# Two-layer transformer on one core: the second attention's preparation reordered and left without scaled output products, and its first head's projections on six PSUM banks shared with VectorE

## The reference, cut to what matters

```python
x = x + _L0_attn_ref(_layernorm(x), ...)
x = x + _L0_ffn_ref(_layernorm(x), ...)
x = x + _L1_attn_ref(_layernorm(x), ...)      # the change is here
x = x + _L1_ffn_ref(_layernorm(x), ...)

def _L1_attn_ref(x, d_kv_w, d_kv_b, u_k_w, u_k_b, u_v_w, u_v_b, d_q_w, d_q_b, u_q_w, u_q_b, qr_w, qr_b, out_w, out_b):
    kv_c = _linear(x, d_kv_w, d_kv_b)
    k_c = _linear(kv_c, u_k_w, u_k_b).reshape(b, s, H, Dh)
    k_r = _linear(kv_c, qr_w, qr_b).reshape(b, s, H, Dr)
    v = _linear(kv_c, u_v_w, u_v_b).reshape(b, s, H, Dh)
    q_c_lat = _linear(x, d_q_w, d_q_b)
    q_c = _linear(q_c_lat, u_q_w, u_q_b).reshape(b, s, H, Dh)
    q_r = _linear(q_c_lat, qr_w, qr_b).reshape(b, s, H, Dr)
    q_r, k_r = _rope(q_r), _rope(k_r)
    q, k = concatenate([q_c, q_r]), concatenate([k_c, k_r])
    probs = softmax(einsum('bhqd,bhkd->bhqk', q, k) / math.sqrt(Dh + Dr))
    ctx = einsum('bhqk,bhkd->bhqd', probs, v)
    return _linear(ctx, out_w, out_b)
```

## Time and profile before

| | |
|---|---|
| time, median of 3 runs | 2518.01 us (2516.64 to 2523.02) |
| the profiled execution | 2521.48 us, its span 2520.2 us |
| mean granted clock of TensorE | 0.972 |
| busy, share of the span | PE 88%, DVE 85%, ACT 74%, POOL 43% |
| start of the preparation, first score, first exponential | 778.4, 867.4, 873.8 us |

### The profile page before, as it was taken

The page is one execution under the profiler, slowest core; times in us unless marked ns, Lnnn a source line. Parts: engine busy times, 40 slices in busy tenths (PEclk is TensorE's granted clock), DMA queues, the critical chain, the costliest instruction groups (busy, mean ns, idle before and its releaser), DMA issues.

```text
span 2520.2 us, 50461 instructions
## 1 busy us (share of the span) xinstructions
PE 2216.9 (88%) x18456; PEld 1584.6 (63%) x18544; DVE 2136.7 (85%) x3174; ACT 1854.4 (74%) x2639; POOL 1074.1 (43%) x1488
## 2 busy tenths in 40 slices
PE   5888888869997599999999999999999999988899
PEld 2444444445555366777777777777777767766587
DVE  6888888758985399999999999999999999988421
ACT  4777777736675388888888888888888888878411
POOL 3312112102222465665665665656656656632200
PEclk9999999979998599999999999999999999999899
DMA  3000000050000099999999999999999999999200
GB/s 126 1 2 2 1 1 2 2 114 1 1 1 1 10 183 187 194 190 193 195 192 190 193 192 192 194 191 193 195 191 191 196 187 193 196 200 196 49 17 17
DMA packets 1119317, 300.67 MB, mean 119 GB/s; under 512 B 1107232, under 2 KB 1116416, under 8 KB 1118208
## 3 DMA queue, kind: packets, MB, share of 16 engines
q1 hardware_dynamic: 1116224, 295.21, 67.4%
q10 hardware_dynamic: 2848, 2.23, 0.3%
HBM read 18.45 MB, written 2.10 MB: 8 GB/s over the span
## 4 chain that ended last, share of the span: by engine, by line
DVE 29%; PE 21%; issue 9%; ACT 4%; DMA 4%; POOL 0%; DVEq 0%; SPq 0%; ACTq 0%; POOLq 0%
DVE parts L1570 13%; DVE lows L1554 12%; DMA partsT<-parts 4%; PE psS L1501 3%; PE psOb L1421 3%; PE psS L1404 2%; PE psS L1406 2%; PE psS L1405 2%; ACT parts L1733 2%; PE psOb L1457 1%; ACT prob L1723 1%; PE psOb L1422 1%; PE psOb L1521 1%; PE psPb L1521 1%; DVE shift L1562 1%
## 5 line engine op out<-in xcount | busy, mean ns | idle before, releaser
L1723 ACT ACTIVATE prob<-psS,shift 128x1024 f32<-128x1024 f32 x512 | 574.4, 1122 | 177.2 <-DVE shift L1562 168.0
L1570 DVE TENSOR_TENSOR parts<-prob,parts 128x1024 f16<-128x1024 f32 x512 | 659.5, 1288 | 23.2 <-ACT parts L1733 20.3
L1554 DVE TENSOR_REDUCE lows<-psS 128x1 f32<-128x1024 f32 x512 | 621.4, 1214 | 8.8 <-PE psS L1406 8.3
L1733 ACT CAST parts<-prob 128x1024 f16<-128x1024 f32 x512 | 538.1, 1051 | 26.0 <-DMA partsT<-parts 22.3
L1404 PE MATMUL psS<-k_hi,q_lo 128*128 128x512 f32 x1024 | 448.2, 438 | 102.6 <-ACT prob L1723 97.5
L1421 PEld LDWEIGHTS psOb<-kv,partsT 128*128 128x128 f16 x4096 | 356.9, 97 | 92.6 <-issue 74.2
L1421 PE MATMUL psOb<-kv,partsT 128*128 128x130 f16 x4096 | 397.5, 221 | 15.4 <-DMA partsT<-parts 15.4
L1406 PE MATMUL psS<-k_hi,q_hi 128*128 128x512 f32 x1024 | 405.3, 396 | 0.0
L1405 PE MATMUL psS<-k_lo,q_hi 128*128 128x512 f32 x1024 | 403.4, 394 | 0.0
L1422 PE MATMUL psOb<-kv,partsT 128*128 128x66 f16 x4096 | 387.2, 192 | 0.0
L1422 PEld LDWEIGHTS psOb<-kv,partsT 128*128 128x128 f16 x4096 | 360.5, 98 | 1.0 <-issue 1.0
(11 more groups left out here) (274 smaller groups left out, 3921.6 us busy)
## 6 DMA issues: line engine op xcount, KB each, us to landing
partsT<-parts SPq DMA_TRANSPOSE x512, 4.9
ef<-in_ewT SPq DMA_DIRECT2D x1, 2048.0 KB, 11.2
rf<-in_rwT SPq DMA_DIRECT2D x1, 2048.0 KB, 10.2
outw_s<-in_outwT SPq DMA_DIRECT2D x1, 2048.0 KB, 9.0
trig<-in_trig SPq DMA_DIRECT2D x2, 1024.0 KB, 11.0
out_x<-ot SPq DMA_DIRECT2D x16, 128.0 KB, 1.7
wug<-in_wupT SPq DMA_DIRECT2D x4, 256.0 KB, 4.1
wug<-in_wgateT SPq DMA_DIRECT2D x4, 256.0 KB, 3.7
```

Of the source, the lines that this page charges most:

```text
L1554: dve.tensor_reduce(lows[:, n % 2, g:g + 1], psS[:, (2 * n + g) % 3, :], AX_X, ALU.min).then_inc(half_min, 1)
L1570: dve.tensor_tensor(parts[:, s, 1, :], prob[:, g, :], parts[:, s, 0, :], ALU.subtract).then_inc(low_done, 1)
L1723: act.activation(prob[:, g, :], psS[:, (2 * n + g) % 3, :], ACT.Exp, bias=shift[:, n % 2:n % 2 + 1], scale=-1.0).then_inc(exp_done, 1)
L1733: act.copy(parts[:, s, 0, :], prob[:, g, :]).then_inc(high_done, 1)
```

## The change

In the preparation:
- The output products are no longer multiplied by `kv_unit`: BT[0], BT[1] and BT[2] are split from `BTf` as it is, and so the first cast (ACT) and the first remainder (DVE) stand between the latent blocks, the second cast ahead of the kv16 casts. The factor is applied where outputs leave PSUM: in ACT's `take_output` and in DVE's `add_output`. `kv_unit` therefore lives in the outer tiles, where its 8 bytes move every tile allocated behind it by 32 bytes in each partition (`parts` from byte 164512 to 164544, `partsT` from 180896 to 180928).
- A root of one column at ACT's start brings the root's table; the real root stands behind the sixth of eight copies of BT, and `fold_hi` behind the rows. DVE fills `wr_hi`, `wr_lo` and the blank head of fold with zeros while it waits for the root.
- The 16 products of `bias_row` come in fours behind each block of latents, those of `beta` behind the last.
- `qr_lo` and `br` come behind the remainders of blocks 0 and 1.

In the first head's projections:
- its pieces go round six banks of psS, and a piece waits for the readers of the piece five before it, not of the one before it.
- DVE, and no more GpSimd, forms the keys' sum and remainder (`first_keys`, `rest_first_keys`). GpSimd keeps those of the queries.
- The first scores wait for the keys block by block.

```diff
+        kv_unit = sb(L, "kv_unit", [P, 2])
...
                     latents(j)
+                    for h in range(4 * j, 4 * j + 4):
+                        pe.matmul(psP[:, 0:D], buv_s[:, h:h + 1].broadcast_to([P, P]), outw_s[:, h, :],
+                                  start=(h == 0), stop=(h == NH - 1))
...
+                def product_rest():
+                    dve.wait_ge(bt_high, 1)
+                    dve.tensor_tensor(BTr, BTf, BT[0], ALU.subtract).then_inc(bt_rest, 1)
...
                     latent_rest(j)
+                    if j < 2:
+                        query_rest(j)
+                    if j == 2:
+                        product_rest()
...
-                dve.wait_ge(bt_scaled, 1)
-                dve.scalar_tensor_tensor(out=BTr, in0=BTf, scalar=kv_unit[:, 0:1], in1=BT[0],
-                                         op0=ALU.mult, op1=ALU.subtract).then_inc(bt_rest, 1)
...
             def scalar():
+                act.wait_ge(scale_ready, 1)
+                act.activation(top_kv[latent, NB:NB + 1], scale_col[latent, 0:1], ACT.Sqrt)
...
+                    if g == 5:
+                        act.wait_ge(var_ready, 1)
+                        act.activation(rstd[:, :], rstd[:, :], ACT.Sqrt).then_inc(root_ready, 1)
...
+        def piece_bank(head, piece):
+            if head:
+                return psP[:, :]
+            return psS[:, piece % 6 // 2, piece % 2 * BANK:(piece % 2 + 1) * BANK]
...
-                if rested_by(head, piece):
-                    pe.wait_ge(rested, rested_by(head, piece))
-                if rotated_by(head, piece):
-                    pe.wait_ge(rotated, rotated_by(head, piece))
+                before = piece if head else piece - 5
+                if before > 0 or head:
+                    if rested_by(head, before):
+                        pe.wait_ge(rested, rested_by(head, before))
+                    pe.wait_ge(rotated, rotated_by(head, before))
...
+                if n == 0:
+                    pe.wait_ge(keys_rested, 2 * (g + 1))
+                    pe.wait_ge(rotated, (6, 7)[g])
+                    pe.wait_ge(rested, 3)
...
-                dve.tensor_tensor(x2[:, n % NT, :], out_bank(n), x2[:, n % NT, :], ALU.add).then_inc(tail_added, 1)
+                dve.scalar_tensor_tensor(out=x2[:, n % NT, :], in0=out_bank(n), scalar=kv_unit[:, 0:1], in1=x2[:, n % NT, :],
+                                         op0=ALU.mult, op1=ALU.add).then_inc(tail_added, 1)
...
+            def first_keys(j):
+                dve.wait_ge(rotated, 2 * j + 2)
+                dve.tensor_tensor(whole_k[rotary, :], rot[0][latent, :], rot[1][latent, :], ALU.add).then_inc(keys_summed, 1)
+
+            def rest_first_keys(j):
+                cols = slice(j * BANK, (j + 1) * BANK)
+                dve.wait_ge(round_done, 2 * j + 2)
+                dve.tensor_tensor(k_lo[0][rotary, cols], whole_k[rotary, :], k_hi[0][rotary, cols].bitcast(F32),
+                                  ALU.subtract).then_inc(keys_rested, 1)
+                dve.wait_ge(keys_rested, j + 1)
+
+            for j in range(NB):
+                rotate(0, 3 * j)
+                rotate(0, 3 * j + 1)
+                if j:
+                    rest_first_keys(j - 1)
+                first_keys(j)
+                rest(0, 3 * j + 2)
+            rest_first_keys(NB - 1)
...
-                act.copy(part[:, :], psO[:, BANK // 2:BANK]).then_inc(out_taken, 1)
+                act.activation(part[:, :], psO[:, BANK // 2:BANK], ACT.Copy, scale=kv_unit[:, 0:1]).then_inc(out_taken, 1)
...
-                for side, (out_rows, rows) in enumerate(((whole, rotary), (whole_k, latent))):
+                for side, (out_rows, rows) in enumerate(((whole, rotary), (whole_k, latent))[:2 if head else 1]):
...
                 rest_queries(0, j, 0)
-                rest_keys(0, j)
```

More of the change, by code:

```diff
@@ L1199, in latent_high @@
                                    bias=blat_s[latent, 0:1]).then_inc(lat_kv, 1)
+                for g in range(2):
+                    act.wait_ge(fold_ready, g + 1)
+                    act.activation(fold_hi[:, 1 + 8 * g:9 + 8 * g, :], six[4 + g][0:C, :].rearrange("p (h c) -> p h c", c=C),
+                                   ACT.Copy, scale=-SCALE).then_inc(fold_high, 1)
                 take_turned(0)
@@ L1627, in scales @@
                                          op0=ALU.mult, op1=ALU.mult).then_inc(mean_ready, 1)
-            for piece in range(12):
-                (rotate, rotate, rest)[piece % 3](0, piece)
+            def first_keys(j):
[15 more added lines that the diff above has]
+            rest_first_keys(NB - 1)
             half(0, 0)
@@ L1851, in rest_keys @@
                                    ALU.subtract).then_inc(rests_done, 1)
-                pool.wait_ge(rests_done, 8 * head + 2 * j + 2)
+                pool.wait_ge(rests_done, sums(head, j) + 2)
             def split(n):
```

106 lines of the change are left out of this document (56 added, 50 removed).

## The result

| | before | after |
|---|---|---|
| median of 4 runs each, us | 2520.52 (2516.64 to 2523.97) | 2500.9 (2497.84 to 2503.9) |
| ratio, 95% interval | | 0.9925 (0.9913 to 0.9936) |
| profiled execution, its span, us | 2521.48, 2520.2 | 2502.4, 2501.1 |
| start of the preparation, first exponential, us | 778.45, 873.80 | 781.98, 851.72 |
| from the one to the other | 95.35 | 69.74 |

The changed kernel is 0.75% faster. Timed again beside the experiments (after_again) it is at 0.9913 (0.9898 to 0.9928), with 69.7 us from start to exponential.

The account below looks back on a forecast made before the run. DVE bounds the loop, which can't get faster; ahead of it a chain of engines sets the first exponential. That comes 25.9 us earlier, less 3.5 paid in the loop: gain 22.4, forecast 2496 us, 8-in-10 range 2487 to 2507.

Parts of the forecast that it names:

- Preparation, front: Preparation up to the first latents: root at 786.4 us, first latents can start at 793.7.
- Preparation, middle: First to last latents: 15.2 us on PE, last latents near 808.5, product_rest done about 810, L1082 at 814.0.
- Preparation, end: L1082 to the first projection: full clock, remainders end at 816.9, first projection 822.4 instead of 831.98; gain so far 9.6.
- First head: First head's projections and scores: blocks of 3.8, 4.5 and 4.5 us, first exponential at 847.9, 25.9 earlier.
- What the loop pays: Output tiles: ACT's copy 0.09 us longer, paid 34 times, 3.1 us; add_output 0.4 us; 3.5 us lost.
- DVE's waits for ACT's high part up from 20.3 by 3 us: Sign expected in the changed profile's loop: these 38 waits, 20.3 us before, grow by 3 us.
- the 34 tiles that it named: Last four output tiles of each odd head and last six of all, where +0.09 us each is paid in full.
- The shift: Rival, chance 0.05: the 32-byte move slows the 512 DMA transposes; 1.5% more each costs 22 us, at 3% 2540.
- The cheap port: Rival, chance 0.22: the port costs little in the first head, blocks of 3.75 us; net gain 25 to 30.
- PE's wait ahead of the first latents costs it the clock: Part of a rival, chance 0.06: idle at 791 to 793.7, latents at half clock; rival's net gain 8 to 14 us.
- the longer copy is paid in most tiles: Rival, chance 0.12: ACT's longer output copy costs 8 to 11 us instead of 3.1; net gain 14 to 18.
- six banks bring nothing: Rival, chance 0.04: first head's blocks stay near 8 us; gain 9.6 less 3.5 or less, 2511 to 2518.

Follow-up runs that it names:

- narrow_last: Changed kernel with beta's one-column products behind the transposes and 13 unread 128x512 products in their place; first exponential 69.3 us after the start, one run, 2496.32 us.
- fixed_unit: Changed kernel with the latents' unit set to the constant 64 instead of measured, and no factor column at the outputs; ratio 0.9894 to the kernel before.
- rest_first: Changed kernel with DVE's rest of a block put ahead of its two key operations; first exponential 69.6 us after the start, one run, 2499.62 us.
- shift_only: Kernel before with two unused columns where kv_unit stands in the changed one, moving later tiles by 32 bytes; ratio 1.0007.

## Why the prediction was right

The forecast was the net gain of 22.4; measured 19.1 between the profiled executions, of which the first layer's 3.53 are chance: 22.6 without it. In medians 19.6 (before came out 2.5 higher than in the runs shown ahead, after 4.9 above the forecast), within the range.

That the first exponential comes 0.3 us from the forecast is in part luck, for misses of up to 1.5 us cancel in the walk: the last latents 1.0 early, the transposes with their remainders 1.45 long, the way from the last rotate to the last keys 0.5 short, the second half of the first scores 0.3 long.

- **Preparation, front.** Root ready, less 3.53, at 786.4 (predicted 786.4), first latents at 793.45 (793.7).
- **Preparation, middle.** Last latents 807.5 (808.5), product_rest done at 809.3 (810), L1082's line at 813.1 (814.0). From the first latents to the last it took 14.0 us, where the prediction added 15.2 (and wrote 808.5 for what is 808.9 by its own sum): it added busy times, and successive lines of PE overlap; L1064's row is 1.88 long and L1074's starts 1.71 behind it. A microsecond better, and lost again at once:
- **Preparation, end.** This step failed: "the last bias products and those of beta keep PE busy until 811.8, so I take the full clock". PE was busy until 811.2 (811.8), then waited 1.95 us, and did the transposes at half clock (3.48 us). narrow_last and fixed_unit show what it hangs on here: with wide products in the place of the narrow ones and a wait of 0.92, or with the narrow ones and no wait, they take 1.94 and 1.97. The remainders end 4.35 behind the line's start instead of 2.9, of which the start, 0.9 early, gives most back: they end at 817.5 (816.9), BT[2] 819.7 (819.2), first projection 822.7 (822.4). Gain 9.3 for 9.6.
- **First head.** The first block's second rotate ends at 826.4 (826.1), and the next three follow in 12.9 (12.8). The conflict of the two engines is there, as derived from the earlier trace rows (where "a whole L1570 longer" was 1.11 us for 1.215): `whole` 1.73/1.52/1.57/1.59 for 1.27, `whole_k` 1.65 for 0.69. What the prediction didn't say is that DVE's op is the one that loses a whole GpSimd operation in blocks 1 to 3, and that q_lo and `k_lo` would meet too (1.10 in block 1, 1.23 for the last keys, and rest_first); its 4.5 a block was a choice between 3.75 and 4.9, and the sum came out right by it: 3.49, 4.94 and 4.49 for 3.8, 4.5 and 4.5. By the section that it cites, with no conflict for such sums, the second and the third would have been 3.75. Last keys at 843.7 (843.7), half clock in the second half of the scores (as predicted), first exponential 848.2 (847.9).
- **A slip without weight.** The "18 us in which PE does 3.65 us of work" are 20 by the earlier trace rows (812 to 831.98).
- **What the loop pays.** 3.5 predicted, 3.4 measured over fourteen executions. `part` 477 ns (467 from the slope of the earlier trace rows), `add_output` 468 (408 before: +0.06 for 0.05). Its own sign, "DVE's waits for ACT's high part up from 20.3 by 3 us", doesn't show in the sum, 20.0 in 38 waits, because other waits, single ones of 0.6 to 4 us most of all, shrank by as much between the two executions. In 28 of the 34 tiles that it named it does show: 10.0 us for 7.4, and 1.9 more in the mean of all fourteen executions, where +0.09 each makes 2.5. So the place is right, and somewhat over half of the cost is found there; where the rest is paid stays open.
- **Rivals.** The shift costs nothing (shift_only). The cheap port is excluded by the durations. That PE's wait ahead of the first latents costs it the clock is excluded too: 2.45 us at 1.00. That the longer copy is paid in most tiles, 8 to 11 us, is outside what 3.4 with 2 either way allows. And that six banks bring nothing falls: they alone bring 11.7 us.

## What to carry to other kernels

- Walk the new order with the durations of the old rows, engine by engine. Where a stretch is a chain, the walk held to within 1.0 us at each of its points here, with single steps off by up to 1.45, and a missed clock or a missed overlap shows as a term that one can measure.
- A step moved into the shade of another engine is only free if that engine's idle time is where it lands. Putting work on DVE beside GpSimd was worth 4 us here, with the conflict paid: two-input SBUF operations of the two stood in line in both orders that were tried.
- A factor may be moved behind a sum only if it is the same for every term of the sum. Here it differed by channel, and moving it to the outputs made the kernel compute something else.
- A scaling that is measured at run time costs a reduction, a chain of small steps and a multiplication on the path, and once more where it is taken back. A power of two known beforehand takes 5 to 8 us less here by the ratios of fixed_unit (0.9894) and of the changed kernel (0.9925 and 0.9913), and some 7 by the traces (3.5 to the first exponential, 3.4 behind it); it holds only while the latents stay in the range that it was chosen for.

## What the runs showed of the hardware

- Sums of two SBUF tensors in f32 on VectorE and on GpSimd exclude each other in both directions. GpSimd: 1.27 alone, up to 1.73 beside DVE. DVE: 0.69 alone, 1.66 beside GpSimd. In the changed kernel GpSimd's casts of 64x512 go from 0.61 to 1.60 and 1.71 us beside DVE's `query_rest` (1024 columns) and 2.71 beside `product_rest` (2048). Beside operations of DVE that read one operand from PSUM (`rest` in rest_first), GpSimd had its 1.27. The Trainium skill's "Advanced Engine Details and Errata" says in its section "GPSIMD Details" that GpSimd conflicts with VectorE's instructions in a two-port mode or with two SBUF inputs, and these runs agree: 1.66 us for 0.69. The prediction cites only its section "VectorE Performance Modes", which names the two-port modes alone.
- A DVE operation with one SBUF tensor could stand in GpSimd's way as well: beside the multiplication of `kvs` (64x2048, 1.29 us in the kernel before) a cast of GpSimd took 1.57 us for 0.61.
- PE shown as busy wasn't always PE that kept its clock: with 32 products of one column in 2.03 us and a wait of 1.95 behind them, the next 16 transposes take 3.5 us (3.58 with four products of 512 columns between and a wait of 0.82); with 13 products of 512 columns in their place and a wait of 0.92, 1.94 us; with the narrow products and no wait, 1.97.
- The instructions alone don't fix where the clock rises: the preparation's first 32 products took 8.78 us in before and 9.80 in shift_only, which differ in addresses only.
- A column as scale makes ACT's 128x256 copy from PSUM 477 ns instead of 373.
